# A four-layer vision stack on one core: both decays of the scan in PSUM, one bank for the rows of B and C, the product with C at the end of its tick

## The chip, the cores and the metric

The kernel runs on one core of a Trainium2 chip. The metric is the device time of one execution in microseconds (us). Before the change the median of three runs is 31,776.09 us (31,771.49 to 31,792.81).

## The reference

The input is 8 images of 56 x 56 pixels with 128 channels, all float32. Layers 0, 2 and 3 are deformable convolutions (each pixel samples 9 points in 4 groups bilinearly from a padded, projected image), layer 1 is a selective state-space scan in four directions. Cut to what matters:

```
# layers 0, 2, 3
xp = x @ w_in + b_in                       # padded: the table that is sampled
h = gelu(batchnorm(depthwise3x3(x)))
offset, mask = h @ w_off + b_off, softmax(h @ w_msk + b_msk)
y = sum over 9 points of mask * bilinear(xp, place + offset)   # 4 groups
x = x + gamma1 * LN(y @ w_out + b_out);  x = x + gamma2 * LN(mlp(x))
# layer 1, 256 inner channels, 16 states, 4 directions
x0 = silu(depthwise3x3(first half of in_proj(LN(x))))
dt, B, C = softplus(...), ..., ...         # from x0, for each direction
h = h * exp(dt * A) + (dt * x0) * B        # one step a pixel, A = -exp(A_logs)
y = sum over the 16 states of h * C
out = x + out_proj(LN(y) * silu(z)), and then an MLP
```

## The kernel before, in words

**Two streams.** One stream is the 24 stages of deformable convolution (3 layers by 8 images, in the order of `stage_order`). A stage has 25 tiles of up to 128 pixels. GpSimd issues one indirect DMA for each tile and sampled point of a group (line 730): it fetches 128 rows of the stage's table in DRAM by 128 indices (`d_idx`) into a slot `d_g`. Twelve such gathers make a "third" of a tile; there are five slots of a third each. VectorE multiplies a third by its weights ("weigh", line 1318), TensorE sums it with matmuls by the identity ("sum", line 1014), and a chain of 21 steps ("ch") makes the output projection, the norms and the MLP for each pair of tiles. "pr" computes indices and weights for four tiles at a time, on which the gathers wait (`idx`, line 1512). "ax", "at" and "ac" load the next stage's image, write its table (line 629 on the queue of SyncE) and convolve; "al" loads weights.

The other stream is layer 1. Its inner channels are two halves h of 128 partitions. The pixels are cut in 7 pieces of 448; with 4 directions that is 28 pieces (`PIECES`), each done for 16 states: 448 ticks an image (`NSTEP`), 3,584 in all. `sig` is the tick within an image, S or x the tick over all images. "h" items (9 an image piece) compute dt, dt*x0 and B's and C's rows in three bfloat16 parts for the next piece, "c" items a 3x3 convolution; "p", "g" and "m" come between the scans of two images.

**A tick of the scan.** TensorE spreads row x of B over the 128 partitions by a matmul into bank `l_pb`, and a row of C into bank `l_pc` (line 965); in tick S these are row S+1 of B and row S-1 of C. VectorE multiplies dt*x0 by B for both halves at once into one of four buffers `l_wk8` to `l_wk11` (line 1299), scans each half along the pixels with its decay exp(dt*A) (line 1287), and multiplies the states by C (line 1305). ScalarE makes the decays (line 781) and copies the last column of the states, the carry that the next piece of the same direction begins with (line 762). TensorE adds the product to the sum over the states in `l_acc` (line 996). The decay of half 0 is in PSUM (bank `l_pm`); those of half 1 are in three buffers in SBUF (`l_wk5`, `l_wk6`), made up to two ticks ahead. The product with C of tick S-1 is the last thing of tick S on VectorE.

**What sets the order.** All five engines read one plan, a list of items that `Planner` writes. It lays the scan's ticks and the gather stream's thirds into each other at a fixed pace: the largest number of scan ticks to a third that forces no more than 40 ticks beyond what no pace avoids. Within an item an engine has a fixed code order, and each engine works its own part of the list strictly in order; semaphores join them. At the end of a stage the planner "drains" what the next stage's first gathers need. The next stage's first group of indices ("pr" of group 0) is begun only when nothing of the next stage's loading, tables and convolution is left in the list (`if not (self.ahead or self.bank or self.loads or self.prep)`).

**PSUM.** The scan has `l_pb`, `l_pc`, `l_pm` of one bank each and `l_acc` of two; the gather stream has `d_p` and `d_pr`. `bank_uses` counts for each bank who uses it in which turn, and the code waits for the turn before.

## Time and profile before

| | before |
|---|---|
| median of 3 runs | 31,776.09 us |
| profiled execution | 31,708.39 us |
| its span in the trace | 31,706.4 us |
| GpSimd busy | 24,065.7 us, 76% |
| VectorE busy | 22,436.1 us, 71% |
| TensorE matmul busy | 23,142.6 us, 73% |
| ScalarE busy | 12,011.1 us, 38% |
| gathers | 21,168 |

A row of groups of instructions has the source line, the engine, the operation, what it writes and reads, the shapes, the count, then busy us in all and the mean ns of one, then the engine's idle time before these instructions and who ended it. Of the GpSimd only the time in an indirect DMA's descriptor work counts as busy; a part of each gather's issue stands as idle time "issue". In a row of the timeline the first number is the start in us from the span's beginning, the second the duration.

### The profile page before, as it was taken

The page shows a single profiled execution, that of the slowest core. Times are in us where ns is not written, and L with a number is a line of the kernel's source. Part 1 is how long each engine was busy: PE and PEld are TensorE (multiplying, and loading weights), DVE is VectorE, ACT ScalarE, POOL GpSimd, SP SyncE. Part 2 cuts the span into 40 slices and gives each one's busy share as a digit, 9 for nine tenths or more (in the row PEclk, how much of TensorE's full clock was granted, in tenths as well). Part 3 has the DMA queues.
Part 4 walks back from the last instruction along what each step waited for, and adds up shares of the span by engine and source line. Part 5 has one row for each costly group of instructions (what it writes and reads, how often), then busy time and mean ns, then how long its engine had stood idle before and what let it go on. Part 6 is the DMA issues. An engine that isn't in the chain of part 4 may idle for free.

```text
span 31706.4 us, 280317 instructions
## 1 busy us (share of the span) xinstructions
PE 23142.6 (73%) x94224; PEld 14718.8 (46%) x94224; DVE 22436.1 (71%) x31704; ACT 12011.1 (38%) x20358; POOL 24065.7 (76%) x21172
## 2 busy tenths in 40 slices
PE   5577778777787778777877777777877787767444
PEld 4444445444544454444544454444444454435333
DVE  1288877888588868887688858886688858885111
...
GB/s 73 73 49 63 51 64 64 56 63 49 71 59 51 62 70 51 62 48 54 71 58 62 49 72 53 58 50 63 56 55 61 50 70 51 49 42 66 62 56 52
...
## 3 DMA queue, kind: packets, MB, share of 16 engines
...
## 4 chain that ended last, share of the span: by engine, by line
POOL 68%; issue 19%; PE 9%; DVE 2%; ACT 1%; DMA 1%; SPq 0%; POOLq 0%; DVEq 0%; ACTq 0%
POOL d_g L730 68%; PE d_pr L1162 2%; PE d_p L1014 2%; PE l_pc L1127 1%; PE d_pr L1049 1%; DVE l_wk L1287 1%; DMA d_xin<-mid 0%; PE d_pr L1216 0%; SPq L629 0%; PE d_pr L1151 0%; DMA mid<-l_xb 0%; PE l_acc L996 0%; PE d_pr L1150 0%; PE l_acc L1119 0%; PE l_pm L1102 0%
## 5 line engine op out<-in xcount | busy, mean ns | idle before, releaser
L730 POOL DMA_INDIRECT d_g<-table,d_idx x21168 | 24065.5, 1137 | 7598.6 <-issue 6427.4
L1014 PE MATMUL d_p<-d_g,c_ident 128*128 128x128 f32 x43200 | 6435.2, 317 | 3171.5 <-DVE d_g L1318 3169.5
L1014 PEld LDWEIGHTS d_p<-d_g,c_ident 128*128 128x128 f32 x43200 | 6233.1, 231 | 4322.7 <-DVE d_g L1318 3235.7
L996 PE MATMUL l_acc<-l_wk,c_ident 128*128 128x448 f32 x14336 | 7229.8, 634 | 456.2 <-DVE l_yx L1276 360.8
L1318 DVE TENSOR_TENSOR d_g<-d_g,d_wt 128x1536 f32<-128x1536 f32 x1776 | 3101.9, 1747 | 4109.0 <-DMA d_g<-table,d_idx 4106.5
L1299 DVE TENSOR_TENSOR l_wk<-l_wk,l_pb 128x896 f32<-128x896 f32 x3584 | 3829.1, 1068 | 1961.8 <-PE l_pb L965 1954.9
L781 ACT ACTIVATE l_pm<-l_wk,l_a 128x448 f32<-128x448 f32 x3584 | 2272.1, 634 | 7709.3 <-DVE l_wk L1287 7703.1
L996 PEld LDWEIGHTS l_acc<-l_wk,c_ident 128*128 128x128 f32 x14336 | 3161.1, 222 | 2514.4 <-issue 2344.2
L1305 DVE TENSOR_TENSOR l_wk<-l_wk,l_pc 128x896 f32<-128x896 f32 x3584 | 3806.7, 1062 | 22.3 <-ACT l_carry L762 14.7
L1287 DVE TENSOR_TENSOR_SCAN l_wk<-l_wk,l_carry 128x448 f32<-128x448 f32 x3072 | 3518.4, 1145 | 0.0
L1287 DVE TENSOR_TENSOR_SCAN l_wk<-l_pm,l_carry,l_wk 128x448 f32<-128x448 f32 x3072 | 3504.8, 1141 | 2.7
L965 PE MATMUL l_pc<-l_spl,c_sel 96*128 96x448 bf16 x3584 | 1423.5, 397 | 1507.9 <-DVE l_wk L1305 1501.8
L781 ACT ACTIVATE l_wk<-l_wk,l_a 128x448 f32<-128x448 f32 x3584 | 2359.2, 658 | 16.4 <-DVE l_wk L1349 2.3
L762 ACT ACTIVATE l_carry<-l_wk 128x2 f32<-128x2 f32 x3584 | 722.2, 201 | 2784.4 <-DVE l_wk L1287 2779.9
L965 PE MATMUL l_pb<-l_spl,c_sel 96*128 96x448 bf16 x3584 | 1404.9, 392 | 392.4 <-DVE l_wk L1299 390.8
L781 ACT ACT_TABLE_LOAD x1181 | 1515.2, 1283 | 20.8
L965 PEld LDWEIGHTS l_pc<-l_spl,c_sel 96*128 96x128 bf16 x3584 | 369.1, 103 | 2264.2 <-DVE l_wk L1305 2120.4
L1162 PE MATMUL d_pr<-d_xt,d_diag 128*128 128x448 f32 x3024 | 1355.3, 592 | 33.9 <-ACT d_xt L889 27.0
L1216 PE MATMUL d_pr<-d_fc,d_ht 128*128 128x128 f32 (+1 forms) x4800 | 911.2, 349 | 558.6 <-ACT d_ht L950 558.5
L1216 PEld LDWEIGHTS d_pr<-d_fc,d_ht 128*128 128x128 f32 (+1 forms) x4800 | 777.9, 244 | 780.7 <-ACT d_ht L950 725.5
L1209 PE MATMUL d_pr<-d_yt,d_fc 128*128 128x256 f32 (+1 forms) x2496 | 733.7, 421 | 496.4 <-ACT d_ht L950 392.7
L1558 DVE BATCH_NORM_STATS2 d_bs<-d_pr 128x6 f32<-128x128 f32 (+1 forms) x1200 | 295.6, 287 | 943.9 <-PE d_pr L1218 735.8
...
## 6 DMA issues: line engine op xcount, KB each, us to landing
d_g<-table,d_idx POOLq DMA_INDIRECT x21168
...
```

The source lines that it names most:

```text
L730: e.indirect_dma_start(out=m.g[Q % SLOTS][:, j, :], out_offset=None, in_=m.table[k % 2], in_offset=bass.IndirectOffsetOnAxis(ap=m.idx[G % ...
L781: e.activation(m.dA0 if h == 0 else m.dA1[x % 3], m.dt[P % 2][:, h, :], ACT.Exp, scale=m.aa[:, kd, h, n:n + 1]).then_inc(s[f"dA{h}"], 1)
L965: return e.matmul(bank[:, 0:448], m.sel[:, row + n:row + n + 1].to_broadcast([96, 128]), m.spl[P % 2][:, :], start=True, stop=True)
L996: ins = e.matmul(m.acc[:, h, 0:448], m.ident[:, :], m.hb[x % 4][:, h, :], start=(n == 0), stop=(n == 15))
L1014: ins = e.matmul(m.p0[:, t % 2 * 128:t % 2 * 128 + 32 * w], m.ident[:, :], m.g[Q % SLOTS][:, w * p:w * p + w, 32 * r:32 * r + 32], start=( ...
L1162: ins = e.matmul(m.r[1][:, 0:448], m.diag[:, j, :], m.xt[:, 8 * c + dy:8 * c + dy + 8, dx:dx + 56], start=(j == 0), stop=(j == 8))
L1209: ins = e.matmul(bank[:, f * 256:f * 256 + nt * n], m.fc1[:, (2 * f2 + f) * 128:(2 * f2 + f) * 128 + 128], m.x1t[:, 0:nt * n], start=True, ...
L1216: e.matmul(bank[0:n, i * 128:i * 128 + 128], m.ht[:, f, i * n:i * n + n], m.fc2[:, f, :], start=(f == 0), stop=False)
L1287: e.tensor_tensor_scan(m.hb[S % 4][:, h, way], dA[:, way], m.hb[S % 4][:, h, way], ini, ALU.mult, ALU.add).then_inc(s["sh"], 1)
L1299: e.tensor_tensor(m.hb[x % 4][:, :, :], m.dtu[P % 2][:, :, :], bc(m.pb[:, 0:448], 1, 2), ALU.mult).then_inc(s["f_pb"], 1)
L1305: e.tensor_tensor(m.hb[x % 4][:, :, :], m.hb[x % 4][:, :, :], bc(m.pc[:, 0:448], 1, 2), ALU.mult).then_inc(s["f_pc"], 1)
L1318: e.tensor_tensor(g, g, wt, ALU.mult).then_inc(s["weighed"], 1)
```

## The change

- Both halves' decays are in PSUM banks of their own, `l_pm` and `l_pc` (`self.dA`). Each is written one tick ahead, after the scan that read the bank before it.
- B's and C's rows take turns in the one bank `l_pb`: B of tick S+1, then C of tick S (new item "sC", at the end of the tick's items), then B of S+2. Each matmul waits until VectorE has read the one before.
- On VectorE a tick is now scan of half 0, scan of half 1, product with B for the next tick; the product with C is an item of its own ("s2") that stands ahead of the next tick's scans, so behind whatever the plan put between.
- The addition of 1 in softplus goes from VectorE (line 1338) to ScalarE as an Identity with a bias, right behind the exponential. In the norm of item "g" ScalarE's square root and VectorE's reciprocal (line 1396) become ScalarE's Ln and Exp(-0.5 x).
- The 16 small products of the bilinear weights of four full tiles (line 1532) become 4 larger ones.
- The next stage's first group of indices may begin when the first two chunks of its convolution are planned (`self.convs`).

```diff
-        for sig in range(-1, NSTEP + 3):
-            tick = [("sB", i, sig - 1)] * (0 <= sig < NSTEP) + [("s", i, sig)]
+        for sig in range(-1, NSTEP + 1):
+            tick = [("s2", i, sig - 1)] * (sig > 0) + [("s", i, sig)]
...
+                tick.append(("sC", i, sig))
             out.append((1.0, tick))
+        out.append((0.0, [("s2", i, NSTEP)]))
...
+            if x[0] == "ac":
+                self.convs.add(x[1:3])
...
-                    if not (self.ahead or self.bank or self.loads or self.prep):
+                    if not self.prep and not self.bank and (k + 1, 1) in self.convs:
                         self.start_prep(k + 1, 0)
...
-        self.dA0, self.dA1 = self.pm[:, 0:448], [wk[5][:, 0, :], wk[5][:, 1, :], wk[6][:, 0, :]]
+        self.dA = self.pm[:, 0:448], self.pc[:, 0:448]
...
+            for h in range(2):
...
+                        e.wait_ge(s["sh"], 2 * S + h + 1)
+                    kd, c = PIECES[(sig + 1) // 16]
+                    e.activation(m.dA[h], m.dt[P % 2][:, h, :], ACT.Exp, scale=m.aa[:, kd, h, n:n + 1]).then_inc(s[f"dA{h}"], 1)
...
+                e.wait_ge(s["sh"], 2 * S + 2)
+                e.activation(m.carry[:, :, sig % 16], m.hb[S % 4][:, :, end], ACT.Copy).then_inc(s["ca"], 1)
...
+                e.activation(m.dt[P % 2][:, :, :], m.e[:, :, :], ACT.Identity, bias=m.one[:, :]).then_inc(s["uu"], 1)
...
-                e.activation(m.rv, m.pm[:, 0:448], ACT.Sqrt, bias=m.eps[:, :]).then_inc(s["f_pm"], 1)
+                e.activation(m.rv, m.pm[:, 0:448], ACT.Ln, bias=m.eps[:, :]).then_inc(s["f_pm"], 1)
+                e.wait_ge(s["f_pm"], J.free("gv", q))
+                e.activation(m.rv, m.rv, ACT.Exp, scale=-0.5).then_inc(s["rvd"], 1)
...
+        elif kind == "sC":
+            x = NSTEP * item[1] + item[2]
+            e.wait_ge(s["f_pb"], J.use["C", x])
+            spread(x, m.pb, 16).then_inc(s["p_pb"], 1)
...
+        elif kind == "s2":
+            _, i, sig = item
+            S = NSTEP * i + sig
+            if sig < NSTEP:
+                e.wait_ge(s["p_pb"], J.full("C", S))
+                e.wait_ge(s["ca"], S + 1)
+                e.tensor_tensor(m.hb[S % 4][:, :, :], m.hb[S % 4][:, :, :], bc(m.pb[:, 0:448], 1, 2),
+                                ALU.mult).then_inc(s["f_pb"], 1)
...
-                    for i in range(0 if half else nt):
-                        ins = e.tensor_tensor(w4[:, i, :, :, 2 * dy + dx], gp(my)[:, i], gp(fx)[:, i], ALU.mult)
+                    if not half:
+                        ins = e.tensor_tensor(w4[:, :, :, :, 2 * dy + dx], gp(my), gp(fx), ALU.mult)
```

VectorE in the first image's scan, before (L1287 are the scans, with the operation's name as the instruction stream has it; L1299 is the product with B, L1305 that with C, L1318 a weigh):

```order
L1305 TENSOR_TENSOR l_wk8<-l_wk8,l_pc 128x896 [waits s_ca,s_p_pc]
L1318 TENSOR_TENSOR d_g3<-d_g3,d_wt0 128x1536 [waits s_g13]
L1287 SCALAR_TENSOR_TENSOR l_wk10<-l_pm,l_wk10 128x448 [waits s_dA0,s_f_pb]
L1299 TENSOR_TENSOR l_wk11<-l_wk3,l_pb 128x896 [waits s_p_pb]
L1287 SCALAR_TENSOR_TENSOR l_wk10<-l_wk6,l_wk10 128x448 [waits s_dA1]
L1305 TENSOR_TENSOR l_wk9<-l_wk9,l_pc 128x896 [waits s_ca,s_p_pc]
L1287 SCALAR_TENSOR_TENSOR l_wk11<-l_pm,l_wk11 128x448 [waits s_dA0,s_f_pb]
L1299 TENSOR_TENSOR l_wk8<-l_wk3,l_pb 128x896 [waits s_p_pb]
```

The same engine near the same place, after (L1269 are the scans, L1281 the product with B, L1289 that with C):

```order
L1289 TENSOR_TENSOR l_wk8<-l_wk8,l_pb 128x896 [waits s_ca,s_p_pb]
L1269 SCALAR_TENSOR_TENSOR l_wk9<-l_pm,l_wk9 128x448 [waits s_dA0,s_f_pb]
L1269 SCALAR_TENSOR_TENSOR l_wk9<-l_pc,l_wk9 128x448 [waits s_dA1]
L1281 TENSOR_TENSOR l_wk10<-l_wk3,l_pb 128x896 [waits s_p_pb]
L1289 TENSOR_TENSOR l_wk9<-l_wk9,l_pb 128x896 [waits s_ca,s_p_pb]
L1269 SCALAR_TENSOR_TENSOR l_wk10<-l_pm,l_wk10 128x448 [waits s_dA0,s_f_pb]
L1269 SCALAR_TENSOR_TENSOR l_wk10<-l_pc,l_wk10 128x448 [waits s_dA1]
L1281 TENSOR_TENSOR l_wk11<-l_wk3,l_pb 128x896 [waits s_p_pb]
L1560 RECIPROCAL d_rs<-d_rs 128x2 [waits s_sqd]
```

The scan of half 1 reads `l_pc` in place of `l_wk5` or `l_wk6`. The product with C of a tick now comes behind its own product with B of the next tick, here with nothing between them, and both wait for the same bank's matmuls (`s_p_pb`).

TensorE in the scan, before (L965 spreads a row, L996 sums over the states, L1014 is a sum of the gather stream):

```order
L965 MATMUL l_pb<-l_spl0,c_sel 128x448 [waits s_f_pb]
L965 MATMUL l_pc<-l_spl0,c_sel 128x448 [waits s_f_pc]
L996 MATMUL l_acc<-l_wk11,c_ident 128x448 [waits s_f_pc]
L996 MATMUL l_acc<-l_wk11,c_ident 128x448
L1049 MATMUL d_pr1<-l_yx,l_diag 128x448 x3
L1014 MATMUL d_p0<-d_g3,c_ident 128x128 [waits s_weighed]
L1014 MATMUL d_p0<-d_g3,c_ident 128x128 x11
L965 MATMUL l_pb<-l_spl0,c_sel 128x448 [waits s_f_pb]
L965 MATMUL l_pc<-l_spl0,c_sel 128x448 [waits s_f_pc]
```

TensorE, after (L967 spreads a row, L992 sums over the states, L1010 is a sum of the gather stream):

```order
L967 MATMUL l_pb<-l_spl0,c_sel 128x448 [waits s_f_pb] x2
L992 MATMUL l_acc<-l_wk10,c_ident 128x448 [waits s_f_pb]
L992 MATMUL l_acc<-l_wk10,c_ident 128x448
L1045 MATMUL d_pr1<-l_yx,l_diag 128x448 [waits s_f_pb,s_brd,s_f_pc,s_f_r1]
L1045 MATMUL d_pr1<-l_yx,l_diag 128x448 x2
L967 MATMUL l_pb<-l_spl0,c_sel 128x448 [waits s_f_pb]
L1010 MATMUL d_p0<-d_g4,c_ident 128x128 [waits s_weighed]
L1010 MATMUL d_p0<-d_g4,c_ident 128x128 x11
L967 MATMUL l_pb<-l_spl0,c_sel 128x448 [waits s_f_pb]
L992 MATMUL l_acc<-l_wk11,c_ident 128x448 [waits s_f_pb]
```

The two rows of a tick stood one behind the other and waited for different banks. Now the sum over the states and the tick's "h" and "c" items stand between them, and both wait for VectorE's last read of one bank (`s_f_pb`).

## Rows read from the trace of the kernel before

**Rows 1.** The page: busy time, share of the span, instructions of each engine.

```profile
PE 23142.6 (73%) x94224; PEld 14718.8 (46%) x94224; DVE 22436.1 (71%) x31704; ACT 12011.1 (38%) x20358; POOL 24065.7 (76%) x21172
```

**Rows 2.** Source line 730: durations min/median/max in ns, and what idle time ended.

```profile
L730 POOL DMA_INDIRECT d_g<-table,d_idx x21168: 938/944/4370, 157.1 to 31663.6; - x200
...
  issue: 6427.4, 21091
  DVE d_idx L1512: 791.7, 8
  PE d_p L1014: 379.4, 69
```

**Rows 3.** Waits of the span: engine, line, waited for, us, times, longest.

```profile
DVE d_g L1318 <- DMA d_g<-table,d_idx: 4106.5, 747, 15.1
DVE l_wk L1299 <- PE l_pb L965: 1954.9, 895, 13.8
```

**Rows 4.** Windows with and without scan: busy us (count) of PE, PEld, DVE, ACT, POOL.

```profile
2000.00:4000.00 2000.00, 1501.52 (x5962) 920.43 (x5961) 1680.27 (x2202) 851.07 (x1473) 1582.79 (x1370) 0.86 0.21 56
...
30000.00:31706.00 1706.00, 757.26 (x3526) 660.52 (x3526) 309.60 (x726) 143.18 (x251) 1192.74 (x1207) 0.65 0.20 55
```

**Rows 5.** Groups by line in the window 2000:4000, VectorE.

```profile
L1299 DVE TENSOR_TENSOR l_wk<-l_wk,l_pb 128x896 f32<-128x896 f32 x296 | 315.9, 1067 | 137.7 <-PE l_pb L965 137.4
...
L1318 DVE TENSOR_TENSOR d_g<-d_g,d_wt 128x1536 f32<-128x1536 f32 (+1 forms) x113 | 197.4, 1747 | 164.2 <-DMA d_g<-table,d_idx 163.9
```

**Rows 6.** Timeline of the window 2500:2560: start, duration, engine, line.

```profile
2506.60 1.75 DVE L1318 TENSOR_TENSOR d_g<-d_g,d_wt 128x1536 f32<-128x1536 f32 x1
...
2507.34 1.82 POOL L730 DMA_INDIRECT d_g<-table,d_idx  x1 [0.30 <-issue]
...
2510.31 1.14 DVE L1287 TENSOR_TENSOR_SCAN l_wk<-l_wk,l_carry 128x448 f32<-128x448 f32 x1
...
2510.72 1.48 POOL L730 DMA_INDIRECT d_g<-table,d_idx  x1 [0.30 <-issue]
...
2516.82 1.06 DVE L1305 TENSOR_TENSOR l_wk<-l_wk,l_pc 128x896 f32<-128x896 f32 x1
...
2517.80 1.14 DVE L1287 TENSOR_TENSOR_SCAN l_wk<-l_pm,l_carry,l_wk 128x448 f32<-128x448 f32 x1
...
2517.94 0.36 PE L965 MATMUL l_pc<-l_spl,c_sel 96*128 96x448 bf16 x1 [0.48 <-DVE l_wk L1305]
...
2517.96 0.94 POOL L730 DMA_INDIRECT d_g<-table,d_idx  x1 [0.30 <-issue]
```

**Rows 7.** Groups by line and shape over the span, VectorE and TensorE.

```profile
L1299 DVE TENSOR_TENSOR l_wk<-l_wk,l_pb 128x896 f32<-128x896 f32 x3584 | 3829.1, 1068 | 1961.8 <-PE l_pb L965 1954.9 <-issue 1.8
L1305 DVE TENSOR_TENSOR l_wk<-l_wk,l_pc 128x896 f32<-128x896 f32 x3584 | 3806.7, 1062 | 22.3 <-ACT l_carry L762 14.7 <-PE l_pc L965 7.4
L1287 DVE TENSOR_TENSOR_SCAN l_wk<-l_wk,l_carry 128x448 f32<-128x448 f32 x3072 | 3518.4, 1145 | 0.0
L1287 DVE TENSOR_TENSOR_SCAN l_wk<-l_pm,l_carry,l_wk 128x448 f32<-128x448 f32 x3072 | 3504.8, 1141 | 2.7
...
L996 PE MATMUL l_acc<-l_wk,c_ident 128*128 128x448 f32 x14336 | 7229.8, 634 | 456.2 <-DVE l_yx L1276 360.8 <-DVE l_yx L1271 94.8
...
L1028 PE MATMUL d_pr<-l_xb,l_xp 128*40 128x448 f32 x896 | 619.2, 824 | 11.6 <-ACT d_pst L900 7.3 <-ACT l_xb L823 4.3
...
L1532 DVE TENSOR_TENSOR d_wt<-d_my,d_cc 128x36 f32<-128x36 f32 x1152 | 153.9, 214 | 0.0
...
L1338 DVE TENSOR_SCALAR l_wk<-l_wk 128x896 f32<-128x896 f32 x224 | 139.1, 621 | 46.4 <-ACT l_wk L813 46.4
```

**Rows 8.** The page: the sums of the gather stream on TensorE.

```profile
L1014 PE MATMUL d_p<-d_g,c_ident 128*128 128x128 f32 x43200 | 6435.2, 317 | 3171.5 <-DVE d_g L1318 3169.5
```

**Rows 9.** Timeline: the last table writes of stage 17 (SyncE's queue), its first gather.

```profile
22297.95 21.36 SPq L629 DMA_DIRECT2D table<-d_pst  x26
...
22376.47 1.00 POOL L730 DMA_INDIRECT d_g<-table,d_idx  x1 [169.97 <-DVE d_idx L1512]
```

153 lines of the change are left out of this document (61 added, 92 removed).

## The prediction

> **What bounds the kernel now.** I read the page's totals first and could not tell from them: GpSimd 76%, TensorE 73%, VectorE 71% [rows 1]. The source line of the gathers tells. All 21,168 gathers stand one behind the other, and 21,091 of them began after nothing but their own issue time, 6427.4 / 21,091 = 0.305 us each. Real waits are only 791.7 us for indices (8 times) and 379.4 us for slots [rows 2]. So the span is 21,168 x (1.137 + 0.305) = 30,520 us of gathers (1.137 is 24,065 us by the count, from [rows 1]), 1,171 us of waits, and some 15 us around them. GpSimd is the bound, though a third of its time is no work: the median gather takes 0.944 us, the mean 1.137 us [rows 1, 2]. The 0.193 us between them, 4,085 us over all, is what there is to win in the gathers.
>
> Where does it come from? Without a scan the mean is 1192.74 / 1207 = 0.988 us, with the scan 1582.79 / 1370 = 1.155 us [rows 4]. The timeline shows how. A weigh (both inputs in SBUF) ran from 2506.60 to 2508.35; the gather that began at 2507.34 ended 0.81 us after it. A half-1 scan (decay and input in SBUF) ran to 2511.45; the gather begun at 2510.72 ended 0.75 us after it. But a gather that began at 2517.96, inside a half-0 scan whose decay is in PSUM, took 0.94 us [rows 6]. So a gather that begins while a VectorE instruction with two SBUF tensors runs is held until that ends, and one beside an instruction with a PSUM operand is not. If such an instruction takes T and gathers begin every P = 1.44 us, it holds them for T x T / 2P on average. For the 3,584 half-1 scans of 1.145 us [rows 7] that is 0.455 us each, 1,630 us; for the 1,776 weighs of 1.747 us [rows 5] 1,880 us. Together 3,510 of the 4,085 us, the rest being left to rarer instructions: the two sizes fit.
>
> The Trainium skill (SBUF — State Buffer, "SBUF: two separate sides") has VectorE and GpSimd share a port pair, an exclusive lock taken by a VectorE instruction with two SBUF inputs, held for the whole instruction, with the later comer fully blocked. The trace agrees on GpSimd's side: held until VectorE's end, then some 0.8 us. By the same rule a half-1 scan that comes second would wait for the gather, up to 0.94 us, and VectorE would win some 0.3 us x 3,584 = 1,100 us too. The trace does not show that: 1145 ns and 0.0 us idle before, against 1141 ns for the PSUM scan [rows 7]. I cost it at nothing; by the rule the first rival below would be sure.
>
> How far is VectorE from being the bound? In the window from 2,000 to 4,000 us GpSimd never waits; VectorE is busy 1,680.3 of 2,000 us [rows 4], and of its 320 us idle 164 go to waiting for gathers and 137 to waiting for the row of B [rows 5], so 19 to other things. In it 296 ticks run [rows 5]; the scan is 3,584 / 296 = 12.1 such windows. Over the span the wait for B is 1,955 us, 0.55 us a tick [rows 3].
>
> **The change, part by part.**
>
> Half 1's decay in PSUM takes away the hold of the 3,584 half-1 scans. From 1,630 us I take 1,500, since instructions that touch share a gather. That is 1,500 / 12.1 = 124 us of each window: GpSimd could then do it in 1,876 us. The scan itself stays at 1.14 us. The instruction orders show that no scan on VectorE reads two SBUF tensors any more.
>
> VectorE's own work falls a little: 224 additions of 0.62 us [rows 7] are 139 us, 11 in a window; the weights' products cost 153.9 us for one half of them [rows 7], so some 306 us in all, and by a quarter of the instructions I take half of it away (bounds 0 and three quarters), 10 us in a window. In a window it is then 1,680 - 21 = 1,659 us busy, plus the 19 us of other idle time: 1,678. The reciprocals lie between the scans, where VectorE has room: nothing. ScalarE's 224 Identities and the second table load beside Ln and Exp fall on an engine that is 38% busy [rows 1]: nothing for themselves, but they can make a decay late; without that cover they cost what they take, 224 x 1 us at most.
>
> The single bank is the price. Let W be VectorE's wait for TensorE and ScalarE in a tick. Between the end of the product with B and the product with C TensorE must now start and finish a row. Start after release 0.06 us and 0.36 us long [rows 6], with the start of VectorE behind it 0.46 us. What covers it is whatever the plan put between. Counted over the changed order, in 14% of the ticks nothing stands there and in 21% less than 0.46 us. TensorE must by then also have done the sum over the states, 4 x 0.634 = 2.5 us at most [rows 7], which fits under scans and product (3.36 us), but one tick in 16 has the projection before it, 4 x 0.824 = 3.3 us [rows 7], and some have convolutions. Tick by tick that gives 600 to 900 us in all, 0.17 to 0.25 a tick. The row of B is the other half. Before, it was released by the last product with B and needed after a scan, the product with C, whatever stood between and one more scan: 3.35 us and more. Now it is released by the product with C and needed two scans later, 2.29 us, and what the plan puts between ticks stands ahead of it on TensorE: a sum of the gather stream is 6435.2 / 1776 = 3.6 us [rows 8]. In 39% of the ticks TensorE has over 2.9 us there. Adding what is over, tick by tick, gives 1,350 us with TensorE's busy time alone and 3,500 us with the waits of TensorE as they stood in this trace; part of those are waits for weighs that waited for gathers, which go when VectorE no longer leads. So between 0.38 and 0.98 a tick; I take 0.55, what it is today [rows 3], the nearest row. ScalarE adds the carry, now needed 1.5 us after the scan instead of a tick later; I take 0.03 (bounds 0 and 0.2). W is then 0.22 + 0.55 + 0.03 = 0.80 us (bounds 0.55 and 1.4).
>
> A window then takes VectorE 1,678 + 296 x 0.80 = 1,915 us against GpSimd's 1,876. VectorE becomes the bound by a little: 85 us won of 2,000, 1,030 us over 12.1 windows.
>
> Ends of stages: the first indices of stages 17, 21, 22 and 23 stood in VectorE's order behind the last weigh of the stage before, and now two thirds ahead of it; those of stage 7 went the other way. But a first gather needs its table too. For stage 17 the last table writes were issued until 22,319.3 and the gather began at 22,376.5, so after 2 us for landing 55 us of the 170 can go [rows 9]. The other three have less after their tables, and stage 7 may cost some. I take 100 us for all (bounds 0 and 300).
>
> **The sum.** 31,708 (the profiled execution) - 1,030 - 100 = 30,580. The median of the runs is 68 us above that execution: 30,650 us.
>
> **The rivals.**
> 1. GpSimd stays the bound everywhere: W at most (1,876 - 1,678) / 296 = 0.67. Then all 1,500 us come through: 31,776 - 1,500 - 100 = 30,180 us. For it: GpSimd never waited in the window and five slots of 12 gathers buffer 86 us. Against it: only 0.67 where today's wait for B alone is 0.55.
> 2. Slower: the two turns in one bank make VectorE and TensorE wait for each other in each tick. From W = (2,000 - 1,678) / 296 = 1.09 us on VectorE needs more than today's window; at 1.3 us a window takes 2,063 us, 12.1 x 63 = 760 us more, less the 100: 32,440 us. For it: TensorE is as busy as VectorE [rows 1] and loses its lead of a tick; counted with its waits B comes to 0.98. Against: those waits are partly the gathers'.
> 3. The holding doesn't go: gathers are held by any VectorE traffic, or another instruction takes over the hold. Then the gathers keep 1.137 us and only the ends of stages move: 31,680 us, or with W over 1.09 more. Against it stands the 0.94 us gather inside a half-0 scan [rows 6].
>
> **Numbers.** A change of 0.2% (64 us) is about what can be told here. My forecast 0.44, rival 1 0.30, rival 2 0.18, rival 3 0.08. Faster: 0.44 + 0.30 + 0.02 of rival 3 = 0.76; the same 0.05; slower 0.18 + 0.01 = 0.19. The range runs from rival 1 with its ends of stages at their best, 30,050, to the lower part of rival 2, 32,050; the forecast's own range is 30,250 to 31,400 (W from 0.67 to 1.05).
>
> **What would show it.** The mean gather falls from 1.155 to about 1.06 us in the scan's windows and its median stays; no gather is held by a scan. VectorE waits for `l_pb` at two lines, some 0.2 us a tick at the product with C and 0.5 at that with B; its wait for gathers falls from 164 us in a window towards nothing, and gathers begin to wait for slots. The forecast is wrong if a window of 296 ticks takes over 2,000 us (rival 2), if gathers still never wait for slots and take 1.37 us from start to start (rival 1), or if the mean gather stays at 1.15 (rival 3).

## The result, and the profile after

The changed kernel takes 31,317.3 us (median of 4 runs, 31,306.7 to 31,333.9) against 31,773.8 us for the kernel before on the same chip: ratio 0.9857, 95% interval 0.984 to 0.9874. It is faster by 1.4%, 456 us; forecast were 3.5%, 1,126 us. The profiled execution took 31,324.5 us, with a span of 31,322.5, so 384 us less than the span before.

The page's busy times, to be read against [rows 1]:

```profile
PE 23254.6 (74%) x94224; PEld 14589.1 (47%) x94224; DVE 22130.8 (71%) x29697; ACT 12528.9 (40%) x20765; POOL 21917.0 (70%) x21172
```

GpSimd is busy 2,149 us less, and yet only 384 us came out of the span. Its source line (as in [rows 2]) says where they went:

```profile
L732 POOL DMA_INDIRECT d_g<-table,d_idx x21168: 938/944/4094, 153.4 to 31279.7; - x200
...
  issue: 6426.5, 20779
  PE d_p L1010: 1447.4, 369
  DVE d_idx L1505: 745.6, 16
  DMA table<-d_pst: 743.9, 4
```

The gathers now wait for slots (1,447 us, before 379) and for tables (744 us, before none). Within the scans alone the waits for slots, added from the gathers' rows, are 945 us against 29: GpSimd is no longer the bound there. VectorE's waits, against [rows 3]:

```profile
DVE d_g L1317 <- DMA d_g<-table,d_idx: 2616.4, 235, 63.7
DVE l_wk L1281 <- PE l_pb L967: 1746.0, 906, 13.0
DVE l_wk L1289 <- PE l_pb L967: 1373.4, 1274, 5.6
```

The wait for gathers fell by 1,490 us; what is left lies outside the scans but for 46 us. A new wait of 1,373 us stands at line 1289, the product with C, where the trace before has 7.4 us [rows 7]. Two views of the window from 2,000 to 4,000 us, the windows and VectorE's groups by line, answer to [rows 4, 5]:

```profile
2000.00:4000.00 2000.00, 1563.78 (x6242) 937.30 (x6241) 1739.43 (x2151) 914.46 (x1559) 1469.17 (x1413) 0.86 0.22 58
```

```profile
L1289 DVE TENSOR_TENSOR l_wk<-l_wk,l_pb 128x896 f32<-128x896 f32 x308 | 333.4, 1082 | 102.6 <-PE l_pb L967 98.2 <-ACT l_carry L778 3.1
L1281 DVE TENSOR_TENSOR l_wk<-l_wk,l_pb 128x896 f32<-128x896 f32 x308 | 329.6, 1070 | 143.2 <-PE l_pb L967 142.3 <-issue 0.6
...
L1317 DVE TENSOR_TENSOR d_g<-d_g,d_wt 128x1536 f32<-128x1536 f32 (+1 forms) x119 | 206.5, 1735 | 0.2
```

308 ticks now fit where 296 did, VectorE waits 0.2 us for gathers, and the mean gather fell from 1.155 to 1469.17 / 1413 = 1.040 us. The timeline shows a gather that begins inside a half-1 scan and is no longer held (before: 1.48 us, [rows 6]):

```profile
2548.49 1.12 DVE L1269 TENSOR_TENSOR_SCAN l_wk<-l_pc,l_carry,l_wk 128x448 f32<-128x448 f32 x1
...
2549.18 0.95 POOL L732 DMA_INDIRECT d_g<-table,d_idx  x1 [0.30 <-issue]
```

It is so throughout, counted from the gathers' and scans' rows of both traces. Of the 3,277 gathers that began inside a half-1 scan before, 2,925 took over 0.98 us (mean of all 1.376 us), and these ended 0.75 us after the scan on average. After, none of 3,058 took so long (mean 0.943 us). Of the gathers that began inside a half-0 scan none did, before or after.

**The ledger.** From the first scan to the last of each image, added over the eight images, the trace before has 23,883 us and the trace after 23,584: 299 us less of the 384. The other 85 us lie before (17), between (26) and behind (42) the scans. Inside them, worked out from VectorE's rows: own work 20,248 to 20,166 (-82); waits for gathers 1,467 to 46 (-1,421); waits for B 1,941 to 1,719 (-222); waits for C 7 to 1,371 (+1,364); waits for the carry +41; smaller waits +21. So the holds went as promised, and the rows of B and C took four fifths of it back.

### The profile page after: what moved, and what is told of

The parts are those of the page before. It is cut to its first block and busy times, and to the rows that moved or that the text cites. A ratio compares the mean times of both kernels' runs of the same rounds, so it can differ in the third digit from the quotient of the medians.

```text
span 31322.5 us, 282005 instructions
## 1 busy us (share of the span) xinstructions
PE 23254.6 (74%) x94224; PEld 14589.1 (47%) x94224; DVE 22130.8 (71%) x29697; ACT 12528.9 (40%) x20765; POOL 21917.0 (70%) x21172
## 5 line engine op out<-in xcount | busy, mean ns | idle before, releaser
L732 POOL DMA_INDIRECT d_g<-table,d_idx x21168 | 21916.8, 1035 | 9363.4 <-issue 6426.5
L992 PE MATMUL l_acc<-l_wk,c_ident 128*128 128x448 f32 x14336 | 7611.5, 663 | 137.4 <-DVE l_yx L1305 99.0
L1010 PE MATMUL d_p<-d_g,c_ident 128*128 128x128 f32 x43200 | 6108.8, 307 | 1937.3 <-DVE d_g L1317 1937.2
L1010 PEld LDWEIGHTS d_p<-d_g,c_ident 128*128 128x128 f32 x43200 | 6127.8, 224 | 2264.5 <-DVE d_g L1317 1637.9
L967 PE MATMUL l_pb<-l_spl,c_sel 96*128 96x448 bf16 x7168 | 2898.7, 404 | 4123.0 <-DVE l_wk L1289 3129.3
L1281 DVE TENSOR_TENSOR l_wk<-l_wk,l_pb 128x896 f32<-128x896 f32 x3584 | 3835.0, 1070 | 1753.5 <-PE l_pb L967 1746.0
L1289 DVE TENSOR_TENSOR l_wk<-l_wk,l_pb 128x896 f32<-128x896 f32 x3584 | 3880.8, 1083 | 1438.7 <-PE l_pb L967 1373.4
L992 PEld LDWEIGHTS l_acc<-l_wk,c_ident 128*128 128x128 f32 x14336 | 3268.0, 229 | 2118.7 <-issue 2031.8
L967 PEld LDWEIGHTS l_pb<-l_spl,c_sel 96*128 96x128 bf16 x7168 | 722.8, 101 | 7355.8 <-DVE l_wk L1289 3582.9
L1269 DVE TENSOR_TENSOR_SCAN l_wk<-l_pm,l_carry,l_wk 128x448 f32<-128x448 f32 x3072 | 3513.5, 1144 | 0.0
L1269 DVE TENSOR_TENSOR_SCAN l_wk<-l_pc,l_carry,l_wk 128x448 f32<-128x448 f32 x3072 | 3457.4, 1125 | 0.0
L773 ACT ACTIVATE l_pc<-l_wk,l_a 128x448 f32<-128x448 f32 x3584 | 2276.1, 635 | 1186.9 <-DVE l_wk L1269 1185.6
L1045 PE MATMUL d_pr<-l_yx,l_diag 128*128 128x448 f32 x2016 | 840.3, 556 | 24.8 <-ACT l_xb L823 11.6
L1158 PEld LDWEIGHTS d_pr<-d_xt,d_diag 128*128 128x128 f32 x3024 | 602.5, 207 | 545.7 <-issue 484.8
```

The lines of the kernel that those rows point to most:

```text
L732: e.indirect_dma_start(out=m.g[Q % SLOTS][:, j, :], out_offset=None, in_=m.table[k % 2], in_offset=bass.IndirectOffsetOnAxis(ap=m.idx[G % ...
L773: e.activation(m.dA[h], m.dt[P % 2][:, h, :], ACT.Exp, scale=m.aa[:, kd, h, n:n + 1]).then_inc(s[f"dA{h}"], 1)
L967: return e.matmul(bank[:, 0:448], m.sel[:, row + n:row + n + 1].to_broadcast([96, 128]), m.spl[P % 2][:, :], start=True, stop=True)
L992: ins = e.matmul(m.acc[:, h, 0:448], m.ident[:, :], m.hb[x % 4][:, h, :], start=(n == 0), stop=(n == 15))
L1010: ins = e.matmul(m.p0[:, t % 2 * 128:t % 2 * 128 + 32 * w], m.ident[:, :], m.g[Q % SLOTS][:, w * p:w * p + w, 32 * r:32 * r + 32], start=( ...
L1045: ins = e.matmul(m.r[1][:, 0:448], m.cdiag[:, 9 * h + j, :], m.grid[:, h, 8 * c + dy:8 * c + dy + 8, dx:dx + 56], start=(j == 0), stop=(j ...
```

## The experiments

The runs fell on chips of two kinds. On three of them the kernel before takes 31,712 to 31,774 us; on four others it takes 34,793 to 35,232 us, and every variant is slower than it. Only the first kind can speak of the measured 1.4%; the second is told of at the end.

| run | time, us | kernel before, us | ratio [95%] |
|---|---|---|---|
| after_b: the changed kernel again | 31,328 | 31,712 | 0.9876 [0.9847, 0.9905] |
| e_before_nohold_b | 31,498 | 31,712 | 0.9931 [0.9908, 0.9953] |
| e_after_sbuf_b | 31,778 | 31,712 | 1.0017 [1.0005, 1.0028] |
| e_mid_b_b | 32,813 | 31,712 | 1.0344 [1.0314, 1.0374] |
| c_early_b | 31,265 | 31,766 | 0.9839 [0.9811, 0.9868] |
| half_acc_c | 31,974 | 31,766 | 1.0064 [1.0041, 1.0087] |
| e_before_nohold | 35,979 | 35,228 | 1.0209 [1.0173, 1.0245] |
| e_after_sbuf | 35,983 | 35,228 | 1.0226 [1.0192, 1.026] |
| e_scan_alone | 36,812 | 35,228 | 1.0459 [1.0426, 1.0493] |
| e_mid_b | 37,590 | 35,228 | 1.0677 [1.0644, 1.0711] |
| own_rows | 36,512 | 34,793 | 1.0489 [1.0459, 1.0519] |
| scan_alone_b | 36,667 | 34,793 | 1.0534 [1.0504, 1.0564] |
| half_acc | 36,807 | 34,793 | 1.0574 [1.0544, 1.0604] |
| c_early | 36,897 | 34,793 | 1.0604 [1.0579, 1.0629] |
| own_rows_b | 36,746 | 35,232 | 1.0429 [1.0354, 1.0504] |
| half_acc_b | 37,093 | 35,232 | 1.0527 [1.0447, 1.0608] |
| own_rows_c | 36,777 | 35,094 | 1.047 [1.0412, 1.0527] |
| fill | 38,543 | 35,094 | 1.0972 [1.0922, 1.1022] |

Names that differ only in the ending _b or _c are the same kernel on another chip; e_scan_alone and scan_alone_b are one kernel too.

> The changed kernel itself beside the kernel before on one chip, to anchor the runs that follow. If the kernel before takes 31,776 us there, 31,317 us within 0.3%. On the chip of the first four experiments the kernel before took 35,228 us; if it is such a chip again, theory A (the changed order waits for TensorE twice in a tick) expects the changed kernel to be slower than the kernel before there, near 36,300 us, since the sum of a slow TensorE and two turns is paid in each tick.

Measured: 31,328 us beside 31,712, as expected. The next three runs were made on the same chip.

**The hold alone, in the order of before (e_before_nohold_b).** Half 1's scan reads half 0's decay in PSUM; half 1's own decay is still made and left unused, so no scan has two SBUF inputs, and order and banks stay. Half 0's next decay waits for both scans.

```
-                    e.wait_ge(s["sh"], 2 * x - 1)
+                    e.wait_ge(s["sh"], 2 * x)
...
-                    dA = m.dA0 if h == 0 else m.dA1[S % 3]
+                    dA = m.dA0
```

> The kernel before with half 1's scan reading half 0's decay in PSUM (half 1's own decay is made and not used), once more. On a chip where the kernel before takes 31,776 us theory A expects 30,300 us (29,900 to 30,700), theory C 31,700 us.

Measured: 31,498 us, 0.9931, so the removed hold gives 213 us there, no more. Theory A's 29,900 to 30,700 fell. Theory C was nearer with its 31,700, and the gathers do wait for slots (1,623 us, before 379), but the hold costs more than the nothing that it said. VectorE's groups of this kernel and the page's row of the gathers:

```profile
L1299 DVE TENSOR_TENSOR l_wk<-l_wk,l_pb 128x896 f32<-128x896 f32 x3584 | 3837.4, 1071 | 3352.9 <-PE l_pb L965 3346.9 <-issue 0.3
L1305 DVE TENSOR_TENSOR l_wk<-l_wk,l_pc 128x896 f32<-128x896 f32 x3584 | 3801.6, 1061 | 38.4 <-PE l_pc L965 19.9 <-ACT l_carry L762 18.0
```

```profile
L730 POOL DMA_INDIRECT d_g<-table,d_idx x21168 | 21983.7, 1039 | 9463.6 <-issue 6346.2
```

The gather's mean is 1,039 ns and the hold is gone, but the wait for B went from 1,955 to 3,347 us. In the scans VectorE's wait for gathers fell by 1,444 us and its wait for B rose by 1,392. Here no bank is shared. So the row of B comes late also where it has its own bank and is spread a tick ahead, once nothing else slows VectorE down.

**The hold put back, in the changed order (e_after_sbuf_b).**

```
-        self.dA = self.pm[:, 0:448], self.pc[:, 0:448]
+        self.dA = self.pm[:, 0:448], wk[5][:, 0, :]
```

> The changed kernel with half 1's decay in a buffer in SBUF, once more. On a chip where the kernel before takes 31,776 us theory A expects 31,450 to 31,950 us with the mean gather near 1,120 ns, theory C within 0.2% of the changed kernel beside it.

Measured: 31,778, which is 450 us or 1.4% over the changed kernel beside it, as theory A had it, and no different from before by more than 0.3%. By its groups and the page:

```profile
L1317 DVE TENSOR_TENSOR d_g<-d_g,d_wt 128x1536 f32<-128x1536 f32 x1752 | 3068.7, 1752 | 3089.6 <-DMA d_g<-table,d_idx 3086.9
```

```profile
L732 POOL DMA_INDIRECT d_g<-table,d_idx x21168 | 23787.4, 1124 | 7940.0 <-issue 6509.8
```

The gather is back at 1,124 ns, and 2,647 of the 3,096 gathers that began inside a half-1 scan took over 0.98 us again. VectorE waits 482 us more for gathers than in the changed kernel, about the whole difference. The new order and the smaller edits with the hold in place are worth nothing; the second decay in PSUM is worth 1.4%, all of what the change gives. Both experiments together: the hold is the cause of the gain, and its size is set by what waits next.

**The product with B between the scans (e_mid_b_b).** Everything is as in the changed kernel, but VectorE runs scan, product with B, scan, so that C's row has a scan to hide under; the carry is copied ahead of half 1's decay.

```
-            if sig + 1 < NSTEP:
-                x = S + 1
...
+                if h == 0 and sig + 1 < NSTEP:
+                    x = S + 1
...
+                if h == 1 and 0 <= sig < NSTEP:
...
+                    e.activation(m.carry[:, :, sig % 16], m.hb[S % 4][:, :, end], ACT.Copy).then_inc(s["ca"], 1)
```

> The changed kernel with the product with B between the two scans and the carry ahead of half 1's decay, once more. On a chip where the kernel before takes 31,776 us theory A expects 30,100 to 30,500 us, with the wait for C under 300 us; theory B (TensorE has no more time) expects within 0.3% of the changed kernel beside it.

Measured: 32,813 us, 1.0344, 4.7% slower than the changed kernel. Theory A fell, and so did theory B, which had the time within 0.3%. VectorE's groups:

```profile
L1290 DVE TENSOR_TENSOR l_wk<-l_wk,l_pb 128x896 f32<-128x896 f32 x3584 | 3876.5, 1082 | 1039.7 <-PE l_pb L967 932.0 <-ACT l_carry L764 92.3 <-issue 0.6
L1282 DVE TENSOR_TENSOR l_wk<-l_wk,l_pb 128x896 f32<-128x896 f32 x3584 | 3848.2, 1074 | 3554.6 <-PE l_pb L967 3551.2
```

C's wait fell by 441 us and B's rose by 1,805. The row of B is released by the product with C and now needed one scan (1.14 us) later, not two; with what TensorE has in hand at that moment it is late in 1,598 ticks, in the changed kernel in 906. C's row gained a scan of room and B's lost one, but the second weighed four times as much. The granted clock was lower too, 0.805 against 0.831; how much of the loss is the clock's doing isn't shown.

**Which ticks wait.** I then sorted the ticks of a trace (from one half-0 scan to the next, without the last of each image and a few over 15 us) by the mean clock granted to TensorE in them: "0.50" are those with a mean under 0.55 (nearly all of the tick at 1.2 GHz), "1.00" those over 0.95 (nearly all at 2.4 GHz), "changing" the rest. Means per tick in us, worked out from the traces:

| kernel, clock in the tick | ticks | length | TensorE busy | wait B | wait C |
|---|---|---|---|---|---|
| before, 0.50 | 300 | 5.66 | 5.30 | 0.55 | 0.01 |
| before, changing | 1,475 | 7.40 | 5.31 | 0.67 | 0.00 |
| before, 1.00 | 1,780 | 6.11 | 4.76 | 0.40 | 0.00 |
| after, 0.50 | 284 | 6.44 | 6.01 | 0.61 | 0.70 |
| after, changing | 1,389 | 6.92 | 5.54 | 0.62 | 0.49 |
| after, 1.00 | 1,883 | 6.23 | 4.59 | 0.34 | 0.26 |
| c_early_b, 1.00 | 1,902 | 6.30 | 4.68 | 0.55 | 0.09 |
| half_acc_c, 0.50 | 846 | 6.11 | 4.96 | 0.56 | 0.23 |
| half_acc_c, changing | 1,923 | 7.11 | 4.95 | 1.05 | 0.22 |
| half_acc_c, 1.00 | 781 | 6.20 | 4.50 | 0.32 | 0.29 |

In the changed kernel a tick at 2.4 GHz waits 0.59 us for the two rows and one at 1.2 GHz 1.31 us. The ticks at 2.4 GHz still have over a third of the whole wait (1,883 x 0.59 = 1,110 of 3,119 us). The table alone doesn't tell cause from effect, as the clock may as well have fallen because TensorE stood waiting. A tick at 0.50 shows the mechanism; first its window (columns as in [rows 4]), then the timeline:

```profile
2911.00:2921.00 10.00, 8.27 (x21) 4.80 (x22) 7.79 (x9) 3.37 (x7) 7.87 (x8) 0.50 0.22 66
```

```profile
2912.73 0.55 PE L967 MATMUL l_pb<-l_spl,c_sel 96*128 96x448 bf16 x1 [2.23 <-DVE l_wk L1289]
...
2913.08 3.19 PE L992 MATMUL l_acc<-l_wk,c_ident 128*128 128x448 f32 x4
...
2914.69 1.06 DVE L1281 TENSOR_TENSOR l_wk<-l_wk,l_pb 128x896 f32<-128x896 f32 x1
...
2916.20 1.86 PE L1032 MATMUL d_pr<-l_bcd,c_mix 8*128 8x448 f32 x2
...
2917.99 0.55 PE L967 MATMUL l_pb<-l_spl,c_sel 96*128 96x448 bf16 x1
...
2918.58 1.09 DVE L1289 TENSOR_TENSOR l_wk<-l_wk,l_pb 128x896 f32<-128x896 f32 x1 [2.18 <-PE l_pb L967]
```

The bank was free for C's row at 2,915.75, when the product with B ended. TensorE was still at the sum over the states (3.19 us for the four parts, against 1.67 in ticks at 2.4 GHz) and then at two matmuls of the hidden layer, 1.86 us; C's row began at 2,917.99 and VectorE stood 2.18 us.

The whole trace of the changed kernel says the same. I took each wait of VectorE for a row that was over 0.1 us and compared the start of the row's matmul with the moment at which its bank came free. In 369 waits, 173 us and all for C, the row began within 0.2 us: that is the bare hand-over. In the other 1,810 (905 for B, 905 for C, together 2,941 us) the row began later. VectorE stood 2,148 us before these rows even began, and in all but 32 us of that TensorE was busy with other matmuls. So the waits are a TensorE that is behind, at either clock: 1,302 of the 1,810 late rows were themselves done at full clock (in under 0.45 us).

**C's row ahead of those matmuls (c_early_b).** One line of the tick moves: TensorE spreads C's row right behind the sum over the states.

```
             if 0 <= sig < NSTEP:
+                tick.append(("sC", i, sig))
                 if 2 <= q <= 10 and j + 1 < len(PIECES):
...
-                tick.append(("sC", i, sig))
```

> The changed kernel with one thing moved: in a tick TensorE spreads C's row right behind the accumulation, ahead of the convolution or hidden-layer matmuls of that tick. Theory T: the wait of the product with C falls from 1,373 us to 500..900, the wait for B stays near 1,750, and the time is 30,700..31,050 on a chip where the kernel before takes some 31,750. Rival L (hand-over): both waits within 150 us of the changed kernel's and the time within 0.3% of 31,328. Rival G (GpSimd takes the time back): the waits fall as in T, but VectorE's waits for gathers rise by as much and the time is above 31,200. On a chip where the kernel before takes 35,000, 36,900 again.

Measured: 31,265 us, 0.9839, in the trace 69 us under the changed kernel. That is the fastest version here, but its interval overlaps the changed kernel's, so a gain over it isn't shown. VectorE's groups:

```profile
L1289 DVE TENSOR_TENSOR l_wk<-l_wk,l_pb 128x896 f32<-128x896 f32 x3584 | 3877.1, 1082 | 724.9 <-PE l_pb L967 642.7 <-ACT l_carry L778 70.8 <-issue 1.9
L1281 DVE TENSOR_TENSOR l_wk<-l_wk,l_pb 128x896 f32<-128x896 f32 x3584 | 3840.2, 1071 | 2368.9 <-PE l_pb L967 2362.5 <-issue 0.4
```

C's wait fell by 731 us, to 643, inside the range of theory T (500 to 900), which shows that half of C's wait was other matmuls ahead of its row; rival L is refuted. But B's rose by 617, where theory T had it stay, and so its 30,700 to 31,050 us was missed as well: TensorE, as late as before, now comes late to B's row. Its order deals the lateness out; it doesn't remove it.

**Less work for TensorE (half_acc_c).** The sum over the states of half 1 is left out in 14 of 16 ticks.

```
-                for h in range(2):
+                for h in range(2 if n in (0, 15) else 1):
```

> The changed kernel with the accumulation of the second half's states left out in 14 of 16 ticks (3,136 ticks, two matmuls of 448 columns fewer in each); all else is as changed. Theory T (the rows come late because TensorE is behind with other matmuls): the waits for B and C together fall from 3,120 us to below 1,900, the scan stretches from 2,948 us per image to below 2,860, and the time is 29,900..30,700. Rival L (the waits are the hand-over from VectorE to TensorE and back): the two waits stay above 2,600 us and the time above 31,000. Rival G (GpSimd is the next bound): the waits for the rows fall, VectorE waits for gathers in the scans again, time 30,700..31,000. All this for a chip on which the kernel before takes some 31,750 us; on one where it takes 35,000, this kernel came to 36,807 and 37,093, and is expected there again.

Measured: 31,974 us, 2.1% slower than the changed kernel, with 3,136 matmuls (6,272 records) fewer. Theory T and rival G fell. The numbers of rival L came true (waits above 2,600 us, time above 31,000), but not its mechanism: the bare hand-over, counted as above, is 293 us of the waits. None had foreseen a slower kernel. Clock, TensorE's busy time, and VectorE's groups:

```profile
core 0: 31965.8 us, clock 0.751
```

```profile
PE 22540.4 (71%) x87952; PEld 14785.9 (46%) x87952; DVE 22147.4 (69%) x29697; ACT 12523.5 (39%) x20765; POOL 21904.1 (69%) x21172
```

```profile
L1289 DVE TENSOR_TENSOR l_wk<-l_wk,l_pb 128x896 f32<-128x896 f32 x3584 | 3877.0, 1082 | 920.2 <-PE l_pb L967 843.8 <-ACT l_carry L778 63.9 <-issue 2.7
L1281 DVE TENSOR_TENSOR l_wk<-l_wk,l_pb 128x896 f32<-128x896 f32 x3584 | 3841.0, 1072 | 2869.2 <-PE l_pb L967 2864.4 <-issue 0.9
```

The granted clock fell from 0.831 to 0.751, so TensorE's busy time fell by 714 us and not by the some 3,700 of the matmuls left out, and only 781 ticks are in the class at 2.4 GHz, against 1,883. The waits for the rows rose from 3,119 to 3,708 us. A shorter queue at a lower clock thus made the rows later, not earlier. The lower clock is the nearest explanation, but it is argued and not shown: no run holds the clock and varies the queue alone. The Trainium skill (TensorE: Matmul & The Clock Gate, "What's actually happening") says that the throttled clock is the default and that activity releases it; the fall of the clock with less work agrees.

**The chips on which the kernel before takes 35 ms.** There the hold was gone as well (mean gather 1,029 ns in c_early), and yet the time was longer. Windows of half_acc, and waits of c_early:

```profile
34120.00:34136.00 16.00, 3.41 (x13) 2.60 (x13) 0.00 (x0) 0.00 (x0) 12.25 (x13) 0.66 0.21 53
34136.00:34176.00 40.00, 0.33 (x1) 0.00 (x0) 0.00 (x0) 0.00 (x0) 27.37 (x29) 0.50 0.18 49
```

```profile
DVE l_wk L1281 <- remote: 3350.2, 592, 52.3
DVE l_wk L1281 <- PE l_pb L967: 1678.6, 772, 25.4
```

In 40 us TensorE executes one matmul, VectorE and ScalarE nothing, and GpSimd gathers at its full pace. Nothing that the trace shows ends such waits. TensorE has 1,392 to 1,992 of them in the twelve traces from these chips, 3.2 to 4.1 ms in all; in the traces of the first kind of chip it has at most 5, of 5 us together. Why these chips do so, and why the kernel before suffers least, is open; the changed kernel itself didn't run on one. What the theories expected of each of these runs, for a chip like the first, and what came is told here together; the times are in the table.

e_mid_b, e_before_nohold, e_after_sbuf and e_scan_alone: all four were expected within 3% of the kernel before or under it; they came 2.1 to 6.8% over it, in the same order as on the other chip where they ran there too (the first two lie within each other's interval).

> The changed kernel with the product with B put between the two scans again, and the carry copied ahead of half 1's decay on ScalarE. Theory A (the row of C, released by the product with B, is what VectorE lacks time for): the wait for C at the tick's end falls from 1,373 us to under 300, since scan 1 now covers it; a scan of an image falls from 2,948 to about 2,800 us and the kernel to 30,100 to 30,500 us. Theory B (TensorE itself has no more time, the wait only shows there): the wait for B grows by what the wait for C loses, and the time stays within 0.3% of the changed kernel's 31,317 us.

> The kernel before, but half 1's scan reads half 0's decay in PSUM (half 1's own decay is still made and not used; half 0's next decay waits for both scans). No VectorE scan holds a gather. Theory A (gathers were held and GpSimd was the bound): the mean gather falls from 1,137 to about 1,065 ns, VectorE's wait for gathers during the scans (about 183 us an image) goes, an image's scan takes 2,800 us in place of 2,985, the kernel 30,300 us (29,900 to 30,700). Theory C (VectorE's and TensorE's order binds the scan in both kernels, the hold costs nothing): 31,700 us, with gathers waiting for slots instead.

> The changed kernel with half 1's decay in a buffer in SBUF, all else as changed. Theory A: half 1's scans hold gathers again, 0.4 us each, mean gather from 1,035 to about 1,120 ns; GpSimd needs about 3,000 us for the gathers of one image's scan, more than VectorE's 2,948, so the kernel is slower by 0.5 to 2%: 31,450 to 31,950 us. Theory C: within 0.2% of 31,317 us, since VectorE is the bound there and GpSimd has time to spare.

> The changed scan alone: the addition of 1, the reciprocals and the 16 small products back on VectorE as before, the next stage's first group of indices begun as before. Theory A: VectorE gets back some 300 us of work in the scans' stretches and 165 between them; the kernel takes 31,450 to 31,750 us, between the two. Theory D (the small edits are the whole gain): 31,776 us or more.

c_early, half_acc and own_rows, and the last two again: 4.3 to 6.0% over. All expectations were for a chip like the first, so these runs decide between none of the theories.

> The changed kernel with one thing moved: in a tick TensorE spreads C's row right behind the product of the states with the identity (the accumulation), ahead of the convolution or hidden-layer matmuls of that tick, not behind them. Everything else is as changed. Theory T (in the scans VectorE waits because other matmuls stand ahead of the two rows in TensorE's queue): the wait of the product with C falls from 1,373 us to 500..900, the wait for B stays near 1,750, the scan stretches shrink from 2,948 us per image by 40..80 us, and the time is 30,700..31,050. Rival L (the waits are the hand-over itself, VectorE to TensorE and back, which no place in the queue shortens): both waits within 150 us of the changed kernel's and the time within 0.3% of 31,328. Rival G (GpSimd takes the time back): the waits fall as in T, but VectorE's waits for gathers rise by as much and the time is above 31,200.

> The changed kernel with the accumulation of the second half's states left out in 14 of 16 ticks, so that TensorE has two matmuls of 448 columns fewer in those ticks (3,136 ticks, some 1.2 us each, about 3,700 us of its 23,255 us); VectorE's, ScalarE's and GpSimd's work is unchanged. Theory T (TensorE's queue): the waits for B and C together fall from 3,120 us to below 1,600, the scan stretches by 100 us or more per image, and the time is 29,700..30,600. Rival L (hand-over): the two waits stay above 2,600 us and the time above 31,100. Rival G (GpSimd is next): the waits fall but GpSimd's gaps in the scans vanish and VectorE waits for gathers again, time 30,600..31,000.

> The changed kernel's order of work, but C's row keeps a PSUM bank of its own, and the scan of the second half reads the first half's decay in PSUM (the second half's decay is still computed, into SBUF, and left unused). So no scan holds a gather and no bank is shared. Theory S (sharing one bank by turns is what costs): the waits for B and C together fall from 3,120 us to below 1,500 and the time to 30,300..30,800. Theory T (TensorE's queue, whatever the bank): the waits stay above 2,500 us together, wherever they stand, and the time is within 0.8% of 31,328, as the kernel before without its holds came to 31,498.

> The changed kernel with the accumulation of the second half's states left out in 14 of 16 ticks (3,136 ticks, two matmuls of 448 columns fewer in each, some 3,700 us of TensorE's 23,255 us); VectorE's, ScalarE's and GpSimd's work is unchanged. Theory T (the rows come late because TensorE is behind with other matmuls): the waits for B and C together fall from 3,120 us to below 1,900, the scan stretches from 2,948 us per image to below 2,860, and the time is 29,900..30,700. Rival L (the waits are the hand-over from VectorE to TensorE and back): the two waits stay above 2,600 us and the time above 31,000. Rival G (GpSimd is the next bound): the waits for the rows fall, VectorE waits for gathers in the scans again, time 30,700..31,000.

> The changed kernel's order of work, but C's row keeps a PSUM bank of its own, and the scan of the second half reads the first half's decay in PSUM (the second half's decay is still computed, into SBUF, and left unused). No scan holds a gather and no bank is shared. Theory S (sharing one bank by turns is what costs): the waits for B and C together fall from 3,120 us to below 1,500 and the time to 30,300..30,800. Theory T (TensorE is behind, whatever the bank): the waits for the two rows stay above 2,300 us together, and the time is 31,000..31,400.

Three kernels ran only there. In own_rows C's row keeps a bank of its own, and both scans read half 0's decay:

```
-        return [("pb", ("C", NSTEP * item[1] + item[2]))]
+        return [("pc", ("C", NSTEP * item[1] + item[2]))]
-        self.dA = self.pm[:, 0:448], self.pc[:, 0:448]
+        self.dA = self.pm[:, 0:448], self.pm[:, 0:448]
```

> The changed kernel's order of work, but C's row keeps a PSUM bank of its own, and the scan of the second half reads the first half's decay in PSUM (the second half's decay is still computed, into SBUF, and left unused). No scan holds a gather and no bank is shared. Theory S (sharing one bank by turns is what costs): the waits for B and C together fall from 3,120 us to below 1,500 and the time to 30,300..30,800. Theory T (TensorE is behind in the half of the ticks in which its clock is at the lower level, whatever the bank): the two waits stay above 2,300 us together, and the time is 31,000..31,400. On a chip where the kernel before takes 35,000: 36,500..36,750 again.

It came to 36,777 us, where 36,500 to 36,750 was expected for such a chip.

In fill TensorE gets more work, ahead of B's row:

```
+                if sig >= 2 and (S - 2) % 16 < 15:
+                    for _ in range(4):
+                        e.matmul(m.acc[:, 0, 448:512], m.ident[:, :], m.ident[:, 0:64], start=False, stop=False)
```

> The changed kernel with four small matmuls (the identity by its first 64 columns, into columns of the accumulation's bank that nobody reads) ahead of the spread of B's row in 15 of 16 ticks: about 13,300 matmuls more, an estimated 0.3 to 0.6 us per tick by the 0.16 us per matmul of 128 columns in the undisturbed part of the trace. In half_acc_c TensorE had 6,272 matmuls fewer and its mean granted clock fell from 0.831 to 0.751, and the time rose by 2%. Theory K (the clock follows what TensorE does, and the waits for the rows follow the clock): here the clock rises above 0.86, the waits for B and C stay below 3,400 us and the time is within 0.7% of 31,328, either side. Rival T (only the queue counts): the clock stays at 0.83, each tick in which TensorE is behind is longer by the fill, and the time is 31,600..32,300.

In scan_alone the smaller edits are undone, as here that of the weights' products:

```
-                    if not half:
-                        ins = e.tensor_tensor(w4[:, :, :, :, 2 * dy + dx], gp(my), gp(fx), ALU.mult)
+                    for i in range(0 if half else nt):
+                        ins = e.tensor_tensor(w4[:, i, :, :, 2 * dy + dx], gp(my)[:, i], gp(fx)[:, i], ALU.mult)
```

> The changed kernel's scans alone: its two decays in PSUM, B's and C's rows by turns in one bank and its order, but the smaller edits undone (the addition of one on VectorE, square root and reciprocal, sixteen small products, the old condition for starting the preparation). Theory: the small edits take about 77 us of VectorE's work and 16 of its instructions per piece out of the path, so that without them the time is 80..250 us above the changed kernel's 31,328, that is 31,400..31,580. Rival: they lie beside GpSimd's work outside the scans and are worth nothing, 31,330 within 0.2%. Second rival: they cost, because Ln and Exp load ScalarE's tables more often, and the time without them is below 31,260.

own_rows came to 36,512 us, 1.0% under c_early on the same chip. Separate banks bring little there, which speaks against sharing as the main cause, but only weakly: c_early has another order on TensorE, and the chip is one of the second kind. Its waits for the two rows cannot be told apart from the standstills. In fill the clock was 0.791, where the nine other runs on chips of this kind with all of the kernel's matmuls have 0.761 to 0.781 and the two of half_acc 0.710 and 0.712. That looks as if the clock went with the work again, but the kernel before, without any filler, has 0.787 to 0.796 there too. Theory K's 0.86 wasn't reached, and the time was the worst of all, 9.7% over before:

```profile
PE 26940.2 (70%) x120976; PEld 18386.7 (48%) x120976; DVE 22210.5 (58%) x29697; ACT 12533.3 (33%) x20765; POOL 21554.5 (56%) x21172
```

TensorE is busy 2,646 us more than in c_early, and the time is 1,646 us longer, on another chip of the same kind. This filler at least bought nothing there. scan_alone_b is 0.6% under c_early on its chip and e_scan_alone 2.3% over e_after_sbuf on its own: what the smaller edits are worth stays open beyond the 82 us that VectorE works less in the scans. On a chip of the first kind none of the three kernels ran.

## Why the prediction was wrong, point by point

**Direction and bound: right.** GpSimd led before; after, VectorE with its waits for TensorE sets the pace of the scans. VectorE's wait for gathers in the window went from 164 to 0.2 us, and the gathers wait for slots.

**The hold of 1,500 us: right.** The gathers that began inside a half-1 scan lost 3,277 x (1.376 - 0.944) = 1,416 us before and nothing after. All of GpSimd's busy time fell by 2,149 us. The rest is mostly gathers that began inside VectorE's instructions of the "h" items: over the median of 0.944 us they took 1,133 us before and 414 after, a gain that the forecast left at nothing; why it is so large isn't shown. The weighs, which stay as they are, were priced too high: 1,880 us forecast, 1,237 by the gathers' rows, so the agreement of the two sizes with 4,085 us was in part luck. e_after_sbuf_b shows that it is the decay's place that does it: with it back in SBUF 1,870 us of busy time came back. The VectorE side of the rule of the Trainium skill (SBUF — State Buffer, "SBUF: two separate sides"), by which 1,100 us more would have been won, isn't seen. Half 1's scan went from 1,145 to 1,125 ns, 61 us over 3,072 scans, and with the decay back in SBUF it takes 1,127 ns, so the decay's place isn't behind these 61 us either.

```profile
L1269 DVE TENSOR_TENSOR_SCAN l_wk<-l_pm,l_carry,l_wk 128x448 f32<-128x448 f32 x3072 | 3513.5, 1144 | 0.0
L1269 DVE TENSOR_TENSOR_SCAN l_wk<-l_pc,l_carry,l_wk 128x448 f32<-128x448 f32 x3072 | 3457.4, 1125 | 0.0
```

In e_after_sbuf_b:

```profile
L1269 DVE TENSOR_TENSOR_SCAN l_wk<-l_wk,l_carry 128x448 f32<-128x448 f32 x3072 | 3463.6, 1127 | 0.0
```

**The step that failed: "1,030 us over 12.1 windows"**, measured 299. In the window itself the forecast was nearly exact: 308 ticks in 2,000 us are 6.49 us each, forecast were 1,915 / 296 = 6.47, and W was (142.3 + 98.2 + 3.1) / 308 = 0.79, forecast 0.80. What failed is that one window stood for all. By image, from the first scan to the last, the time changed by -62, +1, -4, -93, -46, -54, -72 and +31 us. Images 1 and 2, where B's wait had been 0.60 and 0.64 us a tick before (0.49 in image 0), won nothing. Over all ticks the 730 us that are missing divide so:
- *The level before* (333 us). In the window a tick took 2,000 / 296 = 6.76 us; over all images it took 23,883 / 3,584 = 6.66. Across the scans VectorE waited 1,467 us for gathers, 121 a window, not 164. The window was worse than the mean, so its gain was too.
- *W, and in it C's term* (277 us). Forecast 0.22 + 0.55 + 0.03 = 0.80 a tick; measured in the scans 0.38 + 0.48 + 0.015 = 0.88. C alone was short by 1,371 - 0.22 x 3,584 = 582 us; B's term was too large by 253, the carry's by 52, so that part of the miss cancelled by luck. C's bounds of 0.17 to 0.25 took the row at full clock, 0.36 us, and the sum over the states at its mean over both levels, 2.5 us, which "fits under scans and product (3.36 us)". At 2.4 GHz C's wait is indeed 0.26. But where the whole tick is at 1.2 GHz the row takes 0.55 and the sum 3.19 us, 3.74 together, and C waits 0.70; in the changing ticks it waits 0.49. These two classes are 47% of all ticks.
- *VectorE's own work and small waits* (120 us). Forecast were 1,659 and 19 us a window, 20,088 and 230 us over 3,584 ticks; measured 20,166 and 273. Of the 254 us less work that the sum has in the scans, 82 came. The product with C rose from 1,062 to 1,083 ns, 74 us.

The forecast's own range doesn't follow from its sum either: W of 0.67 and 1.05 give 30,176 and some 31,540 us, not 30,250 and 31,400.

**Ends of stages, -100:** 85 us came outside the scans, but not by the mechanism named. The four gaps of [rows 9]'s kind, ahead of the first gathers of stages 17, 21, 22 and 23, grew from 634 to 838 us, and three of them are now ended by the table's transfers. VectorE's work outside the scans fell by 223 us, of which 165 are the reciprocals that the forecast put at nothing; that this is where the 85 us come from isn't shown. The first gathers of stages 17 and 21:

```profile
21983.00 0.94 POOL L732 DMA_INDIRECT d_g<-table,d_idx  x1 [164.43 <-DMA table<-d_pst]
...
27497.66 0.94 POOL L732 DMA_INDIRECT d_g<-table,d_idx  x1 [367.98 <-DMA table<-d_pst]
```

**The rivals.** The first (GpSimd stays the bound) is refuted by the gathers' waits for slots. The second named the right place, the rows' turns, and the wrong size: W stayed under 1.09. The bare hand-over is 173 of the 3,119 us; the rest is TensorE being behind when a bank comes free. What isn't settled is whether C's row, in a bank of its own, would have been spread before TensorE fell behind: e_before_nohold_b has B's row late without sharing (0.93 us a tick), c_early_b shows other matmuls in the way, and own_rows, which takes the sharing away, ran only on chips of the second kind. The third is refuted by the mean gather in the window, 1.040 us, and by e_after_sbuf_b.
